# Causal mask of query tiles 2 and 3 moved from TensorE to VectorE, stack reads by quads of heads, and five unrolled orders, in a transformer block on one core

## The reference

```python
qkv = x @ Wqkv + bqkv
scores = jnp.einsum('bhid,bhjd->bhij', q, k) * scale + alibi_causal_bias(s, NUM_HEADS)
attn = jax.nn.softmax(scores, axis=-1)
out = jnp.einsum('bhij,bhjd->bhid', attn, v) ... @ Wo + bo
x = _layernorm(x + out)
wu, wg, wd = ternary_quant(W_up), ternary_quant(W_gate), ternary_quant(W_down)  # mean(|W|), round, clip
hidden = jax.nn.silu(x @ wu.T) * (x @ wg.T)
x = _layernorm(x + hidden @ wd.T)
```

## Time and profile before

| | us |
|---|---|
| median of 3 runs (lowest, highest) | 645.5 (643.96, 646.14) |
| the profiled execution's own time | 643.29 |
| its span, first to last instruction | 641.5 |

### The profile page before, as it was taken

The page is one execution under the profiler, slowest core; times in us unless marked ns, Lnnn a source line. Parts: engine busy times, 40 slices in busy tenths (PEclk is TensorE's granted clock), DMA queues, the critical chain, the costliest instruction groups (busy, mean ns, idle before and its releaser), DMA issues.

```text
span 641.5 us, 13208 instructions
## 1 busy us (share of the span) xinstructions
PE 588.2 (92%) x4282; PEld 355.1 (55%) x4322; DVE 493.0 (77%) x1015; ACT 304.8 (48%) x543; POOL 295.6 (46%) x492
## 2 busy tenths in 40 slices
PE   6277899999999999999999999999999999998694
PEld 3143356674656656674656656574656656573443
DVE  4266968987699868987699868987699868985554
ACT  1045443476235743376235753376335753377151
POOL 0126783264534654265433654255533654255223
PEclk9597999999999999999999999999999999999888
DMA  8954056403860056402860056402860057402001
GB/s 204 306 170 124 2 164 199 100 2 91 229 172 1 1 193 196 102 1 80 231 165 16 1 176 207 108 1 68 232 173 18 1 173 210 108 1 66 2 0 34
DMA packets 48096, 69.43 MB, mean 108 GB/s; under 512 B 4784, under 2 KB 44208, under 8 KB 44976
## 3 DMA queue, kind: packets, MB, share of 16 engines
q1 hardware_dynamic: 48080, 69.22, 37.7%
HBM read 39.59 MB, written 29.36 MB: 107 GB/s over the span
## 4 chain that ended last, share of the span: by engine, by line
PE 72%; DVE 10%; DMA 8%; issue 4%; ACT 2%; SPq 1%; POOL 1%; another core or an unknown queue 0%; POOLq 0%; DVEq 0%; ACTq 0%
PE ring L551 17%; PE max_bank L474 11%; PE acc L504 9%; PE ring L491 8%; PE acc L564 8%; PE ring L454 6%; DMA k_stack<-k_slots 5%; PE max_bank L476 4%; PE ring L459 2%; DVE neg_max L720 2%; PE ring L529 2%; PE ring L513 2%; DMA k_slots<-qk_parts 2%; PE ring L538 1%; DVE z L753 1%
## 5 line engine op out<-in xcount | busy, mean ns | idle before, releaser
L720 DVE TENSOR_REDUCE neg_max<-max_bank 128x1 f32<-128x384 f32 (+3 forms) x352 | 215.9, 636 | 36.2 <-PE max_bank L476 33.8
L606 ACT ACTIVATE probs<-ring 128x512 f32<-128x512 f32 x320 | 171.5, 602 | 99.5 <-PE ring L491 48.3
L841 POOL TENSOR_SCALAR_AFFINE_SELECT probs<-probs 128x256 f32<-128x256 f32 (+1 forms) x320 | 121.6, 407 | 99.1 <-ACT probs L606 99.0
L474 PE MATMUL max_bank<-k_stack,q_stack 112*128 112x384 bf16 (+3 forms) x512 | 132.3, 307 | 21.2 <-DMA k_stack<-k_slots 15.6
L871 POOL TENSOR_TENSOR hidden_lo<-hidden,hidden_hi 128x512 f16<-128x512 f32 x64 | 74.0, 1158 | 121.6 <-ACT hidden_hi L636 121.6
L476 PE MATMUL max_bank<-causal,ident_bf 128*128 128x128 bf16 x512 | 100.7, 224 | 0.0
L491 PE MATMUL ring<-q_stack,k_stack 128*128 128x128 bf16 (+3 forms) x472 | 91.2, 295 | 3.7 <-DMA q_stack<-max_parts 2.9
L625 ACT ACTIVATE gating<-ring,tanh_scale 128x512 f32<-128x512 f32 x64 | 44.0, 687 | 85.2 <-PE ring L551 85.2
L474 PEld LDWEIGHTS max_bank<-k_stack,q_stack 112*128 112x128 bf16 x512 | 50.6, 99 | 59.9 <-DVE neg_max L720 19.9
L504 PE MATMUL acc<-probs,v_ones 128*32 128x512 f32 (+3 forms) x1024 | 78.2, 437 | 1.4 <-POOL probs L841 1.0
L454 PE MATMUL ring<-x_t,wqkv 128*128 128x512 f32 x128 | 63.8, 623 | 3.7 <-DVE x_t L680 3.6
(11 more groups left out here) (89 smaller groups left out, 825.2 us busy)
## 6 DMA issues: line engine op xcount, KB each, us to landing
q_stack<-qk_scratch SPq DMA_DIRECT2D x16, 768.0 KB, 6.0
k_stack<-k_slots SPq DMA_DIRECT2D x16, 768.0 KB, 8.1
qk_scratch<-qk_parts SPq DMA_DIRECT2D x16, 384.0 KB, 5.2
k_slots<-qk_parts SPq DMA_DIRECT2D x16, 384.0 KB, 2.5
xin<-x_dram SPq DMA_DIRECT2D x9, 512.0 KB, 8.2
qk_scratch<-qk_parts SPq DMA_DIRECT2D x16, 256.0 KB, 2.8
k_slots<-qk_parts SPq DMA_DIRECT2D x16, 256.0 KB, 2.4
res<-x_dram SPq DMA_DIRECT2D x8, 512.0 KB, 3.8
```

The lines of the kernel that those rows point to most:

```text
L474: pe.matmul(o, q_stack[0:MAX_ROW, 4 * g + h, P * tile:P * (tile + 1)], k_stack[0:MAX_ROW, 4 * g + h, 0:width], start=True, stop=False)
L606: rg.drained(act.activation(probs[:, g % 2, n, :], rg.bank(step)[:, :], ACT.Exp), step)
L720: dve.tensor_reduce(neg_max[:, g, first_col:first_col + 4 * (len(heads) - 1) + 1:4], max_bank[k][:, 0:width * len(heads)].rearrange("p (h ...
L841: return pool.affine_select(out=v, in_=v, compare_op=ALU.is_ge, fill=0.0, base=0, pattern=([[0, blocks]] if blocks > 1 else []) + [[1, P]] ...
```

## The change

- Mask: for query tiles 2 and 3 (MASK_BY_DVE = 2) the matmul of L476 is left out. The DVE instruction of such a take is then a tensor_tensor_reduce: it computes minus scores minus mask with a wide mask tile (`causal_wide`, 128x512 bf16), writes it back to the PSUM bank, and gives the minimum, which is the negated maximum. Tiles 0 and 1 stay as they were.
- Stack read: four steps, one per quad, each 384 KB of q_stack and 384 KB of k_stack, each with its semaphore; max.g.0 waits for its own quad.
- Weights: three load steps in the order 0, 2, 1, with a semaphore each, abs_sum.i waits for its own. wsum is the last step of the first list, and the three ternary steps, now all on DVE, are in the list of the second iteration.
- Lists: FIRST, SECOND (iteration 1), LOOP (iterations 2 to 6), SEVENTH (iteration 7), LAST. All are written anew. The ring of PSUM banks is counted over the lists. Which sequence a step belongs to is now computed per step (iteration_offset).

The diff, cut; of the new orders only where the steps named above stand in the loop:

```diff
+LOWEST_START = 3e38
+MASK_BY_DVE = 2
...
-            mm = pe.matmul(o[:, width - P:width], ident_bf[:, :], causal[:, :], start=False, stop=True)
+            mm = pe.matmul(o, q_stack[0:MAX_ROW, 4 * g + h, P * tile:P * (tile + 1)],
+                           k_stack[0:MAX_ROW, 4 * g + h, 0:width], start=True, stop=tile >= MASK_BY_DVE)
+            if tile < MASK_BY_DVE:
+                mm = pe.matmul(o[:, width - P:width], ident_bf[:, :], causal[:, :], start=False, stop=True)
...
+    if tile >= MASK_BY_DVE:
+        dve.sem_inc(dve_passed, 1)
+        scores = max_bank[k][:, 0:width]
+        dve.tensor_tensor_reduce(
+            scores, scores, causal_wide[:, SEQ - width:SEQ], -1.0, LOWEST_START, ALU.add, ALU.min,
+            neg_max[:, g, first_col:first_col + 1]).then_inc(max_drained[k], 1)
+        continue
...
-    stack[0:DATA_ROWS, HEADS // 2 * half:HEADS // 2 * (half + 1), :].rearrange("p h n -> p (h n)"),
-    slots_of(t).rearrange("s (d h) n -> d s (h n)", d=DH)).then_inc(stack_in[half], 16)
+    stack[0:DATA_ROWS, 4 * g:4 * g + 4, :].rearrange("p h n -> p (h n)"),
+    by_row[:, :, 4 * quad:4 * quad + 4, :].rearrange("d s h n -> d s (h n)")).then_inc(stack_in[g], 16)
...
-    act.wait_ge(weights_in[3], 48)
+    act.wait_ge(ffn_weights_in[i], 16)
...
-    elif kind == "ternary" and step[1] < 2:
+    elif kind == "ternary":
...
-        body(FIRST, 0)
-        with eng.Fori(1, BATCH) as it:
-            body(LOOP, it)
-        body(LAST, BATCH)
+        for name in ("FIRST", "SECOND"):
+            body(name, FROM[name])
+        with eng.Fori(FROM["LOOP"], FROM["SEVENTH"]) as it:
+            body("LOOP", it)
+        for name in ("SEVENTH", "LAST"):
+            body(name, FROM[name])
```

More of the change, by code:

```diff
@@ L70, in piece, with iteration_offset @@
                 return n, col
-def of_batch_before(step):
-    return step[0] == "exp" and step[1] == 3 or step[0] in ("pv", "nt", "nt_out") and step[1] >= 2
+def iteration_offset(step):
+    name, n = step[0], step[1] if len(step) > 1 else 0
+    if name == "exp" and n == 3 or name in ("pv", "nt", "nt_out") and n >= 2:
+        return -1
+    return 0 if name in NOW_STEPS else -1
+NOW_STEPS = ("tx", "load_next", "qk", "qk_out", "split", "part_write", "stack_read", "v", "v_out", "max", "take", "mt", "mt_out",
+             "exp", "pv", "nt", "nt_out", "load_weights", "abs_sum", "wsum", "ternary")
 RING_STEPS = ("tx", "qk", "v", "at", "x1t", "up", "gate", "mt", "nt", "exp", "wsum")
@@ L98 @@
[L98 to L102 removed]
+    tx.0 tx.1 qk.0 qk.1 qk_out.0 v.0 split.0 part_write.0.0 part_write.0.1 part_write.0.2 qk.2 qk_out.1
@@ new lines @@
+    exp.3.6 exp.3.7 exp.3.8 qk.1 nt.2 exp.3.9 qk_out.1 nt_out.2 qk.2 part_write.0.0 at.0 pv.3.0 pv.3.1
+    part_write.0.1 split.1 pv.3.2 pv.3.3 v.0 nt.3 load_res v.1 nt_out.3 part_write.1.0 part_write.0.2 part_write.2.0
+    at.1 v_out.0 wo.0.0 part_write.1.1 v_out.1 wo.0.1 part_write.1.2 split.2 stack_read.0 wo.1.0 wo.1.1 max.0.0
+    max.0.1 qk.3 part_write.2.1 take.0.0 max.0.2 take.0.1 ln1 stack_read.1 max.0.3 v.2 part_write.3.0 x1t.0 take.0.2
+    x1t.1 take.0.3 v_out.2 x1_lo.0 x1_lo.1 part_write.2.2 v.3 v_out.3 split.3 part_write.3.1 max.0.4 take.0.4 up.0
@@ new lines @@
+    max.0.5 gate.0 take.0.5 max.0.6 swish.0 take.0.6 max.0.7 take.0.7 up.1 max.0.8 swiglu.0 up.2 take.0.8 max.0.9
+    swish.1 gate.1 max.0.10 hidden_hi.0 gate.2 take.0.9 take.0.10 max.1.0 up.3 down.0 mt.0 swish.2 up.4 take.1.0
+    swiglu.1 max.1.1 swiglu.2 load_next max.1.2 mt_out.0 gate.3 hidden_hi.1 max.1.3 swish.3 hidden_hi.2
+    part_write.3.2 take.1.1 take.1.2 swish.4 up.5 max.1.4 gate.4 take.1.3 stack_read.2 max.1.5 take.1.4 down.1
+    swiglu.3 max.1.6 take.1.5 down.2 max.1.7 exp.0.0 exp.0.1 swish.5 take.1.6 hidden_hi.3 max.1.8 swiglu.4 up.6
@@ L426, in _, with body @@
         def _(pe):
-            def body(steps, it):
-                rg = Ring(steps, it)
-                prev = it - 1
-                first = isinstance(it, int) and it == 0
-                for step in steps:
-                    kind = step[0]
+            def body(name, it):
+                rg = Ring(name, it)
+                for step in STEPS[name]:
+                    kind, b = step[0], it + iteration_offset(step)
+                    first = isinstance(b, int) and b == 0
                     if takes_bank(step):
```

345 lines of the change are left out of this document (188 added, 157 removed).

## The result

| | before | after |
|---|---|---|
| median us (lowest, highest; 4 runs each) | 644.81 (643.96, 646.14) | 638.82 (637.01, 638.96) |
| the profiled execution's own time | 643.29 | 638.93 |
| its span | 641.5 | 637.2 |

The ratio is 0.9899, with a 95% interval of 0.9872 to 0.9926: the change makes the kernel 1.0% faster, 6.0 us by the medians and 4.4 us by the two profiled executions. The forecast was 21 us. I cut the span of both traces at the same places: the transposes of x that open each iteration, and the first up matmul of the last iteration.

The account below looks back on a forecast made before the run. It took PE to bound the loop turns, with DVE close behind, and transfers and short dependences the first list. -12.8 + 1.7 - 9.6 - 0.5 = -21.2 us from 643.3 gave 622.1, forecast as 623.5 with 1.4 added; range 611 to 640.

Parts of the forecast that it names:

- Mask matmuls: Each iteration on PE: 32 of 64 mask matmuls leave at 57 ns each, 1.8 us, all on the path in the loop.
- DVE instruction: 32 takes per iteration become a two-input operation with a running minimum: 0.08 us extra each, 2.6 us of DVE per iteration.
- A: Takes in every iteration: the extra per take is large, 0.3 us; DVE becomes the bound, +23.4 us, about 668; chance 0.06.
- B: Takes in every iteration: the extra per take is 0.2 us as on ScalarE; -4.0 us, about 641; chance 0.12.
- Where DVE's work goes: Loop turn behind the stack's arrival: quads make that stretch 4.2 us longer, so DVE has 47.3 us in 51.2, 92% as before.
- The turn: One loop turn: -1.8 us for the mask, +0.2 for somewhat more waiting, so -1.6, from 72.5 to 70.9; bounds -2.4 and 0.
- First list: Start to the second iteration: -4.0 us until max.0.0 and -8.8 after it, together -12.8; bounds -8 and -17.
- Part (b): First list from max.0.0 to its end: PE 36.5 us plus 7 us of stalls, put at 43.0 instead of 51.8, -8.8.
- Second iteration: It gets all three quantisations on DVE, 73.5 us of DVE work with no waiting; put at 74.0 us, +1.7; bounds 0 and +6.
- rival D: Second iteration: the first list's gain is handed on, DVE-bound from end to end, 80 us, +7.7; about 629.5; chance 0.10.
- Iteration 7: Counted with iterations 2 to 7, six at -1.6 us each, -9.6 in all.
- Rival C: Loop: the quads don't come sooner, PE waits 3 us more in each of six turns, +18, about 641; chance 0.08.

Follow-up runs that it names:

- e1: The changed kernel with the mask of all four query tiles back on PE: 646.28 us, ratio 1.0014 to the kernel before, turns of 73.08 us.
- e6b: The changed kernel with the maxima of query tile 3 taken over keys 128 to 511 only, less DVE work: 634.76 us, turns of 71.6 us.
- e9: The changed kernel with the old order in the loop and last iteration, stack read by quads, mask on DVE: 638.82 us, ratio 0.9891 to the kernel before.
- e15: The kernel of e9 with the masks of tiles 2 and 3 on PE again: 639.91 us.

## Why the prediction was wrong

The sign and the range held, the size did not: 638.8 where 623.5 was said. Two steps failed above all: a sum of busy times was taken for the time of the second iteration, and the new order of the steps was given no price beyond 0.2 us of waiting. Step by step:

- **Mask matmuls**: right in price. 32 of them at 57 ns are 1.8 us, and from e1 to the changed kernel PE's busy sum falls by 1.7 a turn (71.8 to 70.1). The step that failed is "all on the path in the loop": in the new order 1.2 are cashed (73.1 to 71.9), in the old order none (72.2 and 72.25 with quads).
- **DVE instruction**: right, and nearer to the lower bound: two instructions, as the Trainium skill (VectorE: DVE Perf Modes, Two Vector instructions with no wait between them) says; the trace agrees, with a row of 140 ns for the second. It costs at most 0.05 us instead of 0.08, since the next operation begins beside it. Rivals A and B are out.
- **Where DVE's work goes**: the step "the stretch behind it is 4.2 us longer" is false, though it explains little of the miss. The four exp units and four pv steps that left the stretch from qk.1 to max.0.0 (the prediction counted three and two) had moved ahead of qk.1, not out of the front: only v.2 had moved behind max.0.0. From the transposes to max.0.0 it is 21.9 us against 22.3 before, and from there to the next transposes 50.0 against 50.4. So DVE's 46.0 us had 48.1 us there, 95%, and not 51.2. I had counted steps between two marks, where I should have counted the PE work in front of the mark. But a DVE with 2.1 us less to do gives only 0.3 a turn (e6b), of the 1.1 that were missed.
- **The turn**: -1.6 forecast, -0.52 measured, within the bounds (-2.4 and 0). By the corners it is made of -0.2 for the quads, +0.9 for the order without the mask and -1.2 for the mask; taken the other way round the table, -0.2, nothing for the mask and -0.4 for the order with it. The term "0.2 for somewhat more waiting" was too small: PE waits 1.3 us a turn for the stack and the maxima (6.3 in five turns), and 0.3 in the kernel before (1.6 in five). The forecast looked for waits at the stack alone; the row of maxima was in none of its terms.
- **First list**: -12.8 forecast, -12.7 measured, with max.0.0 at 24.76 where 24.5 was said. Part (b) took 42.9 us where 43.0 was said. Some of this is luck. The sum 36.5 + 7 gives 43.5, not 43.0. The 1.8 us of the mask in (b) did not come: with the mask back on PE (e1) the part takes 42.8 us. And the trace before spent 10.2 us of (b) in two further stretches at half clock, that of the changed kernel none. No run separates the new order of this list from the moved ternary work, so what made the 8.9 us of (b) is not shown.

```profile
24.76 0.29 PE L539 MATMUL max_bank<-k_stack,q_stack 112*128 112x128 bf16 x1 [9.07 <-DMA k_stack<-k_slots]
```

- **Second iteration**: +1.7 forecast, +8.9 measured, outside the bounds of 0 and +6; rival D's 80 us, given 0.10, is what came. But not for D's reason, DVE-bound from end to end: DVE is idle for 8 us there, and with its ternary work left out the order takes the same time. The step that failed is "With no waiting at all 73.5; I put 74.0": I took a sum of busy time for the time, with two engines above 90%. The runs show that the work costs 6.1 us in the loop's order (at least 4.4 without the half clock), and that the order which hides it costs nearly as much, 5.5. Of the +8.9, some 1.4 us are the stretch at half clock.
- **Iteration 7**: -1.6 forecast, +2.4 measured. Its order costs 1.5 us over the loop's; the rest is that the loop's order stands 0.9 us above the kernel before here. That is the order's too, and not LAST's: with the old order and quads, and the same LAST, the stretch takes 95.1 us (e9) and 94.9 (e15), against 94.9 before.
- **Rival C** is out: the wait ahead of max.0.0 in the loop is 1.2 us in the first turn and 0.6 to 0.8 after it, where 3 more were said. The end agrees with its -0.5, but no more can be said of it: it takes 31.5 to 33.1 us in the traces that have the same LAST.

The misses are 7.2 for the second iteration, 5.4 for the loop, 4.0 for iteration 7 and 0.3 for the rest: 16.9 of the 21.2 us.

## What to carry to other kernels

In this kernel one engine is busy 98% of a turn and its neighbour 92% of the stretch in question, with two buffers between them; work moved from the first to the second was cashed only where the order of both was rewritten, and the rewritten order cost most of it again in waits for transfers. Price the order as a term of its own, with bounds on both sides. A sum of busy times is a floor and not a forecast: with two engines over 90%, ask where each long instruction of the second stands in its queue, and what short one stands behind it. And what is taken out of a start-up stage has to be done somewhere: price it in the place where it lands by what is held back there, not by that engine's average idle time.
